# A two-layer mixture-of-experts image tower on one core: middle groups' rows given out two ahead, difference matrices one ahead, and a later wait on VectorE

## The chip, the cores and the metric

One NeuronCore of one Trainium2 chip runs the whole program. The metric is the device time of one execution in microseconds (us), taken as the median over runs of the same kernel on the same chip. The engines of the core each run their own instruction stream: TensorE (PE, with its weight loads PEld), VectorE (DVE), ScalarE (ACT), GpSimd (POOL) and SyncE (SP), which here only gives out transfers. ScalarE and GpSimd give out transfers too. The streams meet in semaphores: an instruction `wait_ge` stands in one engine's stream until another engine or a transfer has counted far enough, and everything behind it in that stream stands as well.

## The reference, cut to what matters

The input is 128 images of 3 x 224 x 224. Each image becomes 64 patches, each projected to 128 numbers, with a class token in front: 65 tokens an image, 8320 tokens in all. Two layers follow, each with a residual attention part and a residual mixture-of-experts part (all after a layer norm):

```
h = tokens(x) * pos_embed
h = h + attention0(norm(h))            # softmax attention within each image
h = h + experts0(norm(h))              # 32 experts, top 2, relu, hidden 128
h = h + attention1(norm(h))            # below
h = h + experts1(norm(h))              # 16 experts, top 2, gelu, hidden 512
```

The second attention is without softmax. For row t of an image it is

```
delta   = cumsum(h)[t] - h[t-1]                      # its norm is the magnitude
context = sum over s <= t of exp(-softplus(k) * (t - s)) * h[s]
result  = abs(norm2(delta) * context)
```

Both sums are matrix products along the token axis: `delta` with a matrix of zeros and ones ("difference"), `context` with a matrix `exp(rate * distance)`.

## The kernel before, in words

**Front stage.** The tokens are taken in 16 groups of 8 images (520 tokens). For each group the patch projection, the attention of layer 0, the router of layer 0 and the writing of every token's row, twice, into per-expert lists in DRAM run as a software pipeline over groups. The lists are written by GpSimd, ten indirect transfers a group (line 2061, "scatter"; semaphores `scattered`).

**Layer 0's experts.** 73 blocks of up to 256 list rows. SyncE and ScalarE each give out a part of each block's weights and rows (lines 597 and 599). The first 8 blocks are loaded before the lists are complete. From block 8 on the loads wait until everything is scattered and until padding rows have been written behind each list (`pads`, lines 566 to 574: SyncE writes 20 of them, ScalarE 8 and then 4; `dispatched`, line 577). PE transposes (line 910) and multiplies (926, 950), DVE applies relu (1813) and the gate (1861), GpSimd scatters the results back to DRAM (2089, semaphores `y_out`).

**Middle stage.** The tokens are taken again in 13 groups of 640, numbered 0 to 12. In this stage three transfers of 640 KB are given out by SyncE for each group g:

- its rows, two per token, as written by layer 0's experts (`rows_landed(g)`: waits until the results of all blocks that this group may need have landed, then for its buffer, `m_free`, counted by the sum of group g-2; line 627). There are two buffers, `yin` (in `x_hi` and `x_lo`). VectorE's `gather(g)` (line 1884) sums the two rows of a token and takes the norm's statistics.
- its difference matrix (`load_difference(g)`, line 658; waits for `delta_ps`, PE's delta product of group g-2; two buffers).
- its distance matrix (`load_distance(g)`, line 652; waits for `m_spread`, counted by ScalarE's `decays(g-1)`, line 1349; one buffer).

Groups' work overlaps. VectorE's `mid_step(g)` holds, in this order: the norm of group g's router input (`r1_apply`, 1462), `powers` (1901 to 1917), `gather(g+3)` (1884 to 1895), `mixed_in(g+1)` and its statistics (1923, 1452), the choice of experts of g (`r2`, 1570 to 1601), the gate of g (`r2_gate`, 1613 to 1617, which waits for ScalarE's exponentials), the ranks (`r3`, 1630, which waits for PE) and the slots (1645). ScalarE in the same step: `r1_x2T`, `absolute(g+1)` (1342), the copy of rows (1137), `normalized(g+2)` (1333), `guessB(g+1)`, `decays(g+2)` (1349, waits for the distance matrix), the exponentials for the router of g (1209, 1210), `squares(g+2)` (1312), `powers`. PE: `r1`, `r2`, `delta(g+2)` (1029, 1032), `r3` (829 to 835), `context(g+2)`. GpSimd then scatters group g's rows into layer 1's lists (2061, ten transfers).

The first middle groups are worked in among layer 0's last blocks: the table `EARLY` (line 412) gives the block at which step g (from -3 to 1) begins, and each engine's list `early` gives the offset of every piece. `LAST` is 1. Steps 2 to 12 follow as a plain loop once layer 0's blocks are done. On SyncE the early pieces are the rows up to group 4 and the matrices up to group 3; the rest is the loop that the diff touches.

**Layer 1's experts.** 81 blocks of up to 256 rows. The first four are loaded when ten groups' rows are in the lists; the rest wait, as in layer 0, for all scatters and for the pads. The last stage sums the two results of a token and stores the output.

Before layer 0's blocks VectorE waits (lines 1960 and 1961) until all scatters of layer 0 have landed, since the middle groups reuse the buffers these read. The first middle piece on VectorE is `gather(0)`, at block 47.

Of the kernel before, what the change touches and what calls it, by code (L numbers as in the profile page):

```python
# [31 lines left out]
GROUPS = 16  # L32
# [5 lines left out]
TILES = 5  # L38
ROWS = GT // TILES
HALF = GT // 2  # L40
TOP = 2
# [17 lines left out]
MG = TOKENS // (TILES * WIDE)  # L59
# [76 lines left out]
L0 = Layer(1, "L0", 32, 128, 256, 2, ROWS, GROUPS, [3, 7, 11, 15], 12, 8, 34)  # L136
# [124 lines left out]
def build(nc, a, out):  # L261
    ctx = ExitStack()
    with ctx:
# [149 lines left out]
        LAST = max(EARLY)  # L413
# [72 lines left out]
        S = {l.name: LayerSignals(sem, halves, l.name) for l in (L0, L1)}  # L486
# [119 lines left out]
        def sp_blocks(sp, l, behind=None):  # L606
            sp.wait_ge(T.tables_ready, 2 * l.turn - 1)
            for n, scattered in enumerate(S[l.name].scattered):
                sp.wait_ge(scattered, 16 * TILES * TOP * len(range(n, l.known, len(S[l.name].scattered))))
            for i in range(l.early):  # L610
                for part_ in range(l.parts):
                    load_part(sp, l, i, 0, part_)
            pads(sp, l, 0, PADS[l.name])
            dispatched(sp, l)

            def load(u, j):
                if l.unroll * j + u >= l.early:
                    load_part(sp, l, u, j, 0)
                    if l.mixed[l.unroll * j + u]:
                        load_part(sp, l, u, j, 2)  # L620
                if behind:
                    behind(l.unroll * j + u)

            rounds(sp, l, load)
# [7 lines left out]
        def _(sp):  # L632
# [10 lines left out]
            def load_rows(g):  # L643
                h, j = g % 2, g // 2
                if j > 0:
                    sp.wait_ge(m_free[h], j)
                sp_group_in(sp, "L0", g, h, yin, m_in[h])

            def load_distance(g):
                if g > 0:  # L650
                    sp.wait_ge(m_spread, g)
                sp.dma_start(m_dist[:, :, :].rearrange("p t c -> p (t c)"), a["distance"][g]).then_inc(dist_in, 16)

            def load_difference(g):
                h = g % 2
                if g > 1:
                    sp.wait_ge(delta_ps, g - 1)
                sp.dma_start(m_delta[h][:, :, :].rearrange("p t c -> p (t c)"), a["difference"][g])\
                    .then_inc(delta_in[h], 16)

            def mid_class(g):

                done = (g + 1) * TILES * WIDE - 1
                return L0.class_of(done // (TILES * ROWS))

            def landed(l, enough):

                for b in range(max(0, enough - NB), enough):
                    sp.wait_ge(K[l.name].y_out[b % NB], K[l.name].y0[b % NB] + 16 * (l.packets(b) + l.tiles_of(b)))

            def rows_landed(g):
                landed(L0, L0.enough(mid_class(g)))
                load_rows(g)
# [11 lines left out]
                    sp.wait_ge(chunk_used[h][c], GROUPS // 2)  # L685
            sp_blocks(sp, L0, among)
            among.left()
            for g in range(LAST + 3, MG):
                if g > LAST + 3:
                    rows_landed(g)  # L690
                load_distance(g)
                load_difference(g)

            def load_end(g, u, j):
                if j > 0:
# [721 lines left out]
        def _(dve):  # L1417
# [508 lines left out]
            def one_of(g):  # L1926

                return g if 0 <= g < MG else None
# [28 lines left out]
            dve.tensor_scalar(kcol[:, 1:2], kcol[:, 1:2], LEAST, -1.0, ALU.max, ALU.mult).then_inc(consts_dve, 1)  # L1957
            dve.memset(rows_mid[2][:, :, :, D:ROW], 0.0)

            for h in range(2):  # L1960
                dve.wait_ge(S["L0"].scattered[h], 16 * TILES * TOP * (GROUPS // 2))
            counts = {}

            def chosen_first(g):
                counts[g] = r2(L1, g, g % 2, g // 2)
# [8 lines left out]
            def early(g):  # L1974
                if g >= 0:
                    yield 0, r1_apply, L1, g, g % 2, g // 2
                if g + 2 >= 0:
                    yield 1, powers, g + 2, one_of(g + 1), g + 3
                yield 2, gather, g + 3
                if g + 1 >= 0:  # L1980
                    yield 3, mixed_in, g + 1
                    yield 3, r1, L1, g + 1, (g + 1) % 2, (g + 1) // 2
                if g >= 0:
                    yield 4, chosen_first, g
                    yield 6, slots_then, g

            among = Among(early)
            expert_blocks(L0, among)
            among.left()
# [186 lines left out]
```

## Time and profile before

| | |
|---|---|
| median of 3 runs | 1150.5 us (1148.85 to 1151.22) |
| profiled execution, first to last instruction (span) | 1146.4 us |
| profiled execution's own time | not given apart from its span; the span lies 4.1 us under the median |
| PE busy | 936.4 us, 82% |
| DVE busy | 876.0 us, 76% |
| POOL busy | 673.3 us, 59% |
| ACT busy | 511.0 us, 45% |
| moved by transfers | 246.60 MB, mean 215 GB/s |
| granted TensorE clock, mean | 0.889 |

The span runs through four stages: the front (0 to about 458 us), layer 0's experts (to about 692 us, with middle steps -3 to 1 in among them), the plain loop of middle steps (to about 848 us) and layer 1's experts (to the end). Shares of busy time are averages over these stages; each has another limit. All times in the rows are us from the span's start unless marked ns.

### The profile page before, as it was taken

Reading aid. Unit: us, or ns where it says so; the run is one execution under the profiler, and the core shown is the slowest. Engines: PE = TensorE matmul, PEld = TensorE weight load, DVE = VectorE, ACT = ScalarE, POOL = GpSimd, SP = SyncE. Lnnn points to the kernel's source line nnn. Section 1 sums busy time; section 2 is a strip of 40 time slices with the busy share of each in tenths; the row PEclk is TensorE's granted clock in tenths of the full one; section 3 lists DMA queues with packets and bytes.
Section 4 is the critical chain, followed back from the end, with each engine's and each line's share of the span. In section 5 each row is a group of like instructions: output and inputs, shape, how many; then the busy total and the mean of one; then the engine's idle time right before and its main releaser. Section 6 shows DMA issues by size and latency. Waiting matters only on the chain.

```text
span 1146.4 us, 21968 instructions
## 1 busy us (share of the span) xinstructions
PE 936.4 (82%) x6140; PEld 789.8 (69%) x6140; DVE 876.0 (76%) x3376; ACT 511.0 (45%) x1358; POOL 673.3 (59%) x622
## 2 busy tenths in 40 slices
PE   6999999999999973476667876566638999999992
PEld 2666676777667663466556765565638999999992
DVE  0588988988898966466678897677866888888883
ACT  1355555445555421111113545555524666656651
POOL 1036667666666633667777577766674545555552
PEclk9999999999999975678897887777759999999996
DMA  9856655666664032487789854455356888889886
GB/s 374 349 181 223 215 192 199 234 219 215 206 230 142 26 85 71 129 220 208 208 245 329 258 166 152 161 178 181 102 197 233 257 259 272 283 268 342 274 300 223
DMA packets 118667, 246.60 MB, mean 215 GB/s; under 512 B 20914, under 2 KB 85936, under 8 KB 112400
## 3 DMA queue, kind: packets, MB, share of 16 engines
q1 hardware_dynamic: 78016, 191.53, 50.6%
q0 software_dynamic: 18592, 34.68, 8.9%
q10 hardware_dynamic: 21936, 18.98, 5.5%
q8 instruction: 49, 0.80, 0.3%
q14 instruction: 74, 0.61, 0.2%
HBM read 201.68 MB, written 45.43 MB: 216 GB/s over the span
## 4 chain that ended last, share of the span: by engine, by line
PE 43%; DVE 22%; DMA 10%; issue 9%; SPq 7%; ACT 5%; POOL 3%; ACTq 1%; DVEq 0%; POOLq 0%
PE ps L950 11%; PE ps L931 9%; PE ps L734 4%; DMA x_hi<-results_L 3%; PE ps L801 3%; PE ps L785 3%; POOL lists_L L2061 2%; SPq L597 2%; SPq L599 2%; SPq L590 2%; DMA x_lo<-results_L 2%; PE ps L727 2%; PE ps L910 2%; PE ps L773 2%; PE ps L751 2%
## 5 line engine op out<-in xcount | busy, mean ns | idle before, releaser
L2061 POOL DMA_INDIRECT lists_L<-rows,slots x250 | 281.0, 1124 | 185.0 <-issue 173.1
L2089 POOL DMA_INDIRECT results_L<-xin x145 | 144.0, 993 | 122.7 <-DVE xin L1861 95.0
L2089 POOL DMA_INDIRECT results_L<-xin,place x146 | 143.8, 985 | 64.3 <-issue 39.5
L734 PE MATMUL ps<-xin,w_emb 128*128 128x512 f32 x292 | 138.2, 610 | 9.7 <-DMA w_emb<-in_w_main 8.6
L950 PE MATMUL ps<-xin,QK 128*128 128x128 f32 x838 | 115.3, 288 | 6.5 <-DVE QK L1813 4.4
L950 PEld LDWEIGHTS ps<-xin,QK 128*128 128x128 f32 x838 | 107.0, 203 | 8.0 <-DVE QK L1813 4.7
L931 PE MATMUL ps<-x_hi,x_lo 128*128 128x256 f32 (+1 forms) x324 | 98.5, 304 | 1.1 <-DVE x_lo L1829 1.1
L910 PE MATMUL ps<-ident,xin 128*128 128x128 f32 x291 | 65.9, 309 | 39.6 <-DMA xin<-lists_L 37.4
L2070 POOL TENSOR_TENSOR x_lo<-xin,x_hi 128x2048 fp32r<-128x2048 f32 x13 | 60.1, 4625 | 63.8 <-ACT x_hi L1118 63.5
L1271 ACT ACTIVATE QK<-ps,xin 128x256 f32<-128x256 f32 x164 | 64.4, 475 | 71.5 <-PE ps L931 71.5
L734 PEld LDWEIGHTS ps<-xin,w_emb 128*128 128x128 f32 x292 | 52.8, 194 | 59.2 <-issue 48.6
L931 PE MATMUL ps<-x_lo,x_hi 128*128 128x256 f32 (+1 forms) x324 | 92.5, 286 | 0.0
L931 PE MATMUL ps<-x_hi 128*128 128x256 f32 (+1 forms) x324 | 92.4, 285 | 0.0
L1835 DVE TENSOR_SCALAR xin<-xin 128x128 f32<-128x128 f32 x291 | 91.6, 361 | 0.6
L950 PE MATMUL ps<-xin,UH 128*128 128x128 f32 x648 | 89.8, 284 | 2.5 <-DVE xin L1861 2.1
L1137 ACT ACTIVATE h0T<-ps 128x256 f32<-128x256 f32 x73 | 27.9, 383 | 129.0 <-PE ps L910 108.3
L950 PEld LDWEIGHTS ps<-xin,UH 128*128 128x128 f32 x648 | 82.1, 198 | 4.0 <-issue 4.0
L1271 ACT ACTIVATE UH<-ps,xin 128x256 f32<-128x256 f32 (+1 forms) x160 | 55.5, 430 | 37.4 <-PE ps L931 37.4
L910 PEld LDWEIGHTS ps<-ident,xin 128*128 128x128 f32 x291 | 38.7, 157 | 47.8 <-DMA xin<-lists_L 44.8
L926 PE MATMUL ps<-h0T,xin 128*128 128x128 f32 (+1 forms) x326 | 59.2, 318 | 14.8 <-ACT h0T L1137 6.0
L926 PEld LDWEIGHTS ps<-h0T,xin 128*128 128x128 f32 x326 | 53.1, 235 | 17.5 <-issue 9.4
L931 PEld LDWEIGHTS ps<-x_hi,x_lo 128*128 128x128 f32 x324 | 63.3, 195 | 1.5 <-DVE x_lo L1829 1.5
(310 smaller groups left out, 2443.1 us busy)
## 6 DMA issues: line engine op xcount, KB each, us to landing
xin<-in_x_main SPq DMA_DIRECT2D x48, 1536.0 KB, 6.8
xin<-in_w_L SPq DMA_DIRECT2D x81, 578.0 KB
xin<-in_w_L SPq DMA_DIRECT2D x98, 128.0 KB
xin<-lists_L SPq DMA_DIRECT2D x64, 132.0 KB
xin<-in_w_L ACTq DMA_DIRECT2D x65, 128.0 KB
xin<-in_difference SPq DMA_DIRECT2D x13, 640.0 KB
xin<-in_distance SPq DMA_DIRECT2D x13, 640.0 KB
x_hi<-results_L SPq DMA_DIRECT2D x11, 640.0 KB, 5.9
```

The lines of the kernel that those rows point to most:

```text
L734: mm = pe.matmul(psE[h], w_emb[:, k, :], xin[h][c][:, n, :], start=(k == 0), stop=False, skip_group_check=True)
L785: mm = pe.matmul(pair[0][0:SEQ, i * D:(i + 1) * D], x1T[h][:, i * SEQ:(i + 1) * SEQ], wv[:, :], start=True, stop=True)
L801: mm = pe.matmul(pair[2][:, c:c + SEQ], V[h][:, i, :], Pr[h][:, i, :], start=True, stop=True)
L910: mm = pe.transpose(ps[:, banks(l, i)[0], q * 128:(q + 1) * 128], xblk[b][:, q, 0:D], ident[:, :])
L926: mm = pe.matmul(bank_h(i, f)[:, of_part], w1, xTb[p2][:, of_part], start=True, stop=True)
L931: mm = pe.matmul(bank_h(i, f)[:, 0:n_in], w[p2][:, cols_f], x[p2][:, 0:n_in], start=(n2 == 0), stop=(n2 == 2), skip_group_check=True)
L950: mm = pe.matmul(o, hTb[p2][:, f, rows_in], w2[:, f * D:(f + 1) * D], start=(f == 0), stop=(f == l.FC - 1))
L1271: ins = act.activation(hTb[p2][:, f, 0:n_in], ps[:, 2 + 2 * p2 + f // 2, f % 2 * l.block:f % 2 * l.block + n_in], ACT.Gelu, bias=b1)
L1835: ins = dve.tensor_scalar(xblk[u][:, q, 0:D], xblk[u][:, q, 0:D], xblk[u][:, q, SPREAD:SPREAD + 1], xblk[u][:, q, MEAN:MEAN + 1], ALU.mult ...
L2061: pool.indirect_dma_start(out=lists[l.name], out_offset=bass.IndirectOffsetOnAxis(ap=slots_of(l, g, h)[:, t, k:k + 1], axis=0), in_=buf[:, ...
L2070: pool.tensor_tensor(x_lo0[:, :, :].rearrange("p k n -> p (k n)"), xin[h][0][:, 0:KS, :].rearrange("p k n -> p (k n)"), x_hi0[:, :, :].rea ...
L2089: pool.indirect_dma_start(out=results[l.name], out_offset=bass.IndirectOffsetOnAxis(ap=where, axis=0), in_=yblk[u][:, q, :], in_offset=Non ...
```

## The change

SyncE's loop over the remaining middle groups gives out its transfers in another order, and each earlier. Before, for g from 4 to 12: rows of g (from 5 on), distance of g, difference of g. After: first rows of 5 and difference of 4; then for g from 4 to 12: rows of g+2, difference of g+1, distance of g. The waits inside each are the same. On VectorE the wait for layer 0's scatters moves from before layer 0's blocks to just before `gather(0)` at block 47.

```
             sp_blocks(sp, L0, among)
             among.left()
+            rows_landed(LAST + 4)
+            load_difference(LAST + 3)
             for g in range(LAST + 3, MG):
-                if g > LAST + 3:
-                    rows_landed(g)
+                if g + 2 < MG:
+                    rows_landed(g + 2)
+                if g + 1 < MG:
+                    load_difference(g + 1)
                 load_distance(g)
-                load_difference(g)
...
-            for h in range(2):
-                dve.wait_ge(S["L0"].scattered[h], 16 * TILES * TOP * (GROUPS // 2))
             counts = {}
+
+            def buffers_free():
+
+                for h in range(2):
+                    dve.wait_ge(S["L0"].scattered[h], 16 * TILES * TOP * (GROUPS // 2))
...
                     yield 1, powers, g + 2, one_of(g + 1), g + 3
+                if g == -3:
+                    yield 2, buffers_free,
                 yield 2, gather, g + 3
```

## Rows read from the trace of the kernel before

**Rows 1.** Line 1884, 700 to 812 us: what it waited for (us, times).
```profile
  DMA x_hi<-results_L: 11.3, 4
  DMA x_lo<-results_L: 9.5, 3
```

**Rows 2.** Chain that ended last, middle loop: start, us, what.
```profile
694.46 1.35 ACT xin L1349
...
696.94 7.92 DMA x_hi<-results_L
...
704.88 0.83 DVE atok L1884
```

**Rows 3.** Timeline of SP: start, us, engine, line, transfer.
```profile
657.31 20.51 SPq L652 DMA_DIRECT2D xin<-in_distance  x2
...
695.83 0.33 SPq L652 DMA_DIRECT2D xin<-in_distance  x1
```

**Rows 4.** Page, transfers by line: count, size, median us to landing.
```profile
x_hi<-results_L SPq DMA_DIRECT2D x11, 640.0 KB, 5.9
```

**Rows 5.** Busy time by stretch: length, PE, PEld, DVE, ACT, POOL, clock, DMA share, GB/s.
```profile
704.88:717.58 12.70, 8.06 (x51) 7.34 (x51) 11.57 (x70) 5.39 (x22) 9.65 (x11) 0.76 0.47 151
688.50:701.94 13.44, 9.15 (x61) 8.57 (x61) 11.72 (x72) 8.43 (x30) 10.32 (x11) 0.75 0.46 146
```

**Rows 6.** Timeline of DVE: gate, ranks and slots of step 2; slots of 9, 10, 12.
```profile
696.63 0.23 DVE L1613 TENSOR_REDUCE gsum<-lgs 128x5 f32<-128x80 f32 x1
...
697.74 0.39 DVE L1630 TENSOR_TENSOR pick<-ps,oh 128x80 f32<-128x80 f32 x2 [0.25 <-PE ps L835]
...
698.72 0.17 DVE L1645 SCALAR_TENSOR_TENSOR slots<-chosen,rank 128x10 uint32<-128x10 f32 x1
...
809.23 0.17 DVE L1645 SCALAR_TENSOR_TENSOR slots<-chosen,rank 128x10 uint32<-128x10 f32 x1
...
824.27 0.17 DVE L1645 SCALAR_TENSOR_TENSOR slots<-chosen,rank 128x10 uint32<-128x10 f32 x1
...
847.63 0.17 DVE L1645 SCALAR_TENSOR_TENSOR slots<-chosen,rank 128x10 uint32<-128x10 f32 x1
```

**Rows 7.** Timeline of PE, step 2: delta, ranks, context.
```profile
692.90 0.80 PE L1029 MATMUL ps<-xin 128*128 128x128 f32 x2 [2.52 <-ACT xin L1333]
...
697.33 0.23 PE L829 MATMUL ps<-ohs,before 128*128 128x80 bf16 x1
...
698.05 0.39 PE L1029 MATMUL ps<-xin,xin 128*128 128x128 f32 x2
```

**Rows 8.** Timeline of POOL: last result of layer 0; scatters of groups 2 and 5.
```profile
691.98 0.98 POOL L2089 DMA_INDIRECT results_L<-xin,place  x1 [0.30 <-issue]
...
705.99 0.97 POOL L2061 DMA_INDIRECT lists_L<-w_emb,slots  x1 [0.30 <-issue]
...
748.00 0.97 POOL L2061 DMA_INDIRECT lists_L<-w_emb,slots  x1 [3.85 <-DVE slots L1645]
```

**Rows 9.** Line 2061, 705 to 865 us: landing of its scatters.
```profile
DMA to landing us min/median/max: 2.3/2.8/8.2
```

**Rows 10.** Chain that ended last, at the start of layer 1's experts.
```profile
862.80 3.49 DMA lists_L<-rows,slots
```

**Rows 11.** Timeline of SP at that start: the pads.
```profile
850.08 13.10 SPq L574 DMA_DIRECT2D lists_L<-padrows  x16
```

**Rows 12.** Timeline of PE at the start of layer 1's experts.
```profile
871.58 0.69 PE L910 MATMUL ps<-ident,xin 128*128 128x128 f32 x2 [4.88 <-DMA xin<-lists_L]
```

**Rows 13.** Timelines of DVE, ACT and SP at the start of layer 0's experts.
```profile
474.25 0.42 DVE L1813 TENSOR_SCALAR QK<-ps 128x256 f32<-128x256 f32 x1 [8.12 <-DMA lists_L<-rows,slots]
...
471.49 5.39 ACTq L574 DMA_DIRECT2D lists_L<-padrows  x8
...
460.42 16.18 SPq L574 DMA_DIRECT2D lists_L<-padrows  x20
```

**Rows 14.** Chain that ended last, at the start of layer 0's experts.
```profile
479.95 2.08 DMA lists_L<-padrows
```

## The prediction

> **What bounds the kernel now.** I read the waits of the middle loop first, then the chain of waits there, then the timelines of SP, DVE, ACT, PE and POOL side by side for one step, and last the two places where an expert stage starts.
>
> In the middle loop VectorE stops once in each of steps 3 to 9, always before line 1884, the sum of the rows of groups 6 to 12. The reader is to see seven waits, 11.3 + 9.5 = 20.8 us together, all for a rows transfer [rows 1]. The chain shows why: `decays` of one step ends (694.46 + 1.35 = 695.81), SyncE then passes its wait, gives out distance, difference and rows within 1.1 us, and the rows, third in line, land at 704.86; the sum starts at 704.88 [rows 2]. So every step holds a loop: sum, statistics, `decays`, three transfers, sum. Nothing but program order on SyncE ties the rows to `decays`. Their buffer has been free since the sum two groups back.
>
> Between slots of group 2 (698.72) and of group 9 (809.23) lie 110.5 us, seven steps of 15.8 us [rows 6]. Without its wait, step 3 holds 12.70 us of VectorE work from one sum to the end of the next `powers` [rows 5]; over the seven steps it is (110.5 - 20.8) / 7 = 12.8 us.
>
> GpSimd follows. It needs 10 sends a group; in the stretch of 12.70 us it makes 11 with 9.65 us busy and 0.3 us between them [rows 5, 8], so some 12.7 us a group. Late in the loop it waits for VectorE's slots, 3.85 us at 748.00 [rows 8]. Behind the loop the whole delay reaches the end: the last scatter is sent at 862.80 and lands 3.49 us later, SyncE's next loads go out, and PE, which had stood 4.88 us, starts again at 871.58 [rows 10, 12]. From there on PE is the bound to the end, so a time saved at this restart is saved at the end.
>
> **The change part by part.**
>
> (a) *Rows two ahead.* After the change the rows of g+2 are given out once the sum of g is done, more than a step before they are needed, where a 640 KB transfer takes 5.9 us to land [rows 4]. All seven waits go: -20.8 us. Bounds: 0 (if something holds SyncE longer than a step) and 20.8; I take 20.8, as the slack is a full step. No instruction is added on SyncE: the same transfers, in another order.
>
> (b) *What is late next.* PE's order in a step is delta, then ranks, then context. In step 2, which had no wait for rows, delta started at 692.90, ran 4.4 us, the ranks followed at 697.33 with nothing between, and VectorE stood before 1630 [rows 6, 7]. So step 2 is the pattern of a step without the row wait, and it lasted 13.44 us, from 688.50 to 701.94 [rows 5], 0.6 more than 12.8. Seven steps of 13.44 are 94.1 us: together (a) and (b) give 110.5 - 94.1 = 16.4. Bounds of (b): 0 and 0.74 a step (against step 3's own 12.70), so (a) and (b) are worth 15.6 to 20.8.
>
> GpSimd at 12.7 us a group stays just under 13.44 and is no bound.
>
> In those steps the clock granted to PE matters: a pair of delta's matmuls took 0.80 us, of the context products behind it 0.39 [rows 7], the two levels of 1.2 and 2.4 GHz. The Trainium skill (TensorE: Matmul & The Clock Gate, "Part 1: The HAM clock gate") says that the slow clock is the default and that sustained activity releases it; by this a loop without the row wait might keep the fast clock. The trace speaks against it: step 2 had no row wait and its delta still ran slow. It stands below as a rival.
>
> (c) *The first distance matrix.* This goes the other way. Before, the distance of group 4 was given out as soon as `decays(3)` was done, as the second of the two transfers of [rows 3] that end at 677.8, and `decays(4)` could run at 694.46 [rows 2]. After the change SyncE must first give out the rows of group 6. Group 6 lies in the third class of layer 0's tokens, which needs all 73 blocks' results in DRAM. The last of these is sent by GpSimd at 691.98 [rows 8]; a scatter lands 2.8 us after its send at the median, 2.3 at least [rows 9]: about 694.8. So SyncE stands from about 659 (657.31 and two more transfers given out) to 694.8, and the distance of 4 is queued behind it. Before, this wait cost nothing, as the rows of 6 were asked for at 696.94 [rows 2].
>
> Then rows 6, difference 5 and distance 4 go out together. Three such transfers took from 695.83 [rows 3] to 704.86 [rows 2], 9.0 us. Distance 4 lands at about 703.8, and `decays(4)` starts 9.3 us later than before. Behind it on ScalarE stand the exponentials for the router, which VectorE's gate at 696.63 awaits. Between the end of `decays` (695.81) and that gate there were 0.8 us [rows 2, 6], with the exponentials in them, so the slack is between 0 and 0.8; I take 0.5. VectorE, GpSimd and all behind come 8.8 us later. Bounds: if the transfer needed only the 5.9 us of [rows 4] after 694.3, `decays` would start 5.7 later, 5.2 on the path; if the five transfers that can then be in flight (rows 7 and difference 6 follow at once) share the rate evenly, 9.0 x 5/3 = 15 us, so 14.8 on the path. I take 8.8, since the three in front are exactly the pattern measured.
>
> The Trainium skill (DMA: Bandwidth & Descriptors, "Queues, rings and completion order") says that each DMA engine consumes the descriptors of a ring in order, so distance 4 would wait for the two in front and not for the two behind. The same page's fit, 2.0 us plus bytes over 436 GB/s ("Anatomy of one DMA"), would be an estimate of 6.5 us for the three instead of the 9.0 measured, and the forecast would be 2.5 us lower; the measured number is used.
>
> (d) *Difference one ahead.* Difference g+1 stands before distance g and waits for delta of g-1. Counted from the start of the sum, step 2's delta ended at 697.33 - 688.50 = 8.8 us and its `decays` at 7.3 [rows 2, 5, 7], so distance g goes out some 2 us later than it could, at about 9.3. It is wanted at the next `decays`, at 13.4 + 6.0 = 19.4, so it has 10.1 us to land. Two transfers in line take between 5.9 (one) and 9.0 (three) [rows 2 to 4]. Cost 0, cover 1 us at least; if it is gone, every step pays (rival 3).
>
> (e) *End of the loop.* Steps 10 to 12 have no sum; from slots 9 to slots 12 they take 38.4 us [rows 6] as before. The last send came 15.2 us after slots 12 [rows 6, 10], GpSimd being behind. After the change it has run dry before slots 10 and starts level: two groups of 12.7 and nine sends of 1.27 put the last send 36.8 us after slots 10 (824.27), which is 13.4 us after slots 12 [rows 6], 1.8 closer. The pads, 850.08 + 13.10 = 863.2 plus 2.1 of landing, then are last, at 865.3 against the old 866.3 [rows 10, 11, 14]. Gain 1.0, bounds 0 and 1.8.
>
> (f) *VectorE's wait.* It was 8.12 us before the first relu [rows 13]. Taking it away lets blocks 0 to 2 run some 5 us earlier. Block 8's loads don't follow: they went out when ScalarE's second set of pads had landed, 479.95 + 2.08 = 482.0 [rows 14], and these stood behind its own first eight, 471.49 to 476.9 [rows 13], not behind VectorE. From there SyncE's issue of loads is the chain. Value 0. Bounds: a gain of 3.4 if the loads could start when SyncE's pads (460.42 + 16.18, plus 2.1) have landed; nothing below 0, since at block 47 the scatters have been in for 100 us.
>
> Sum: -16.4 + 8.8 - 1.0 = -8.6 us. The profiled span of 1146.4 becomes 1137.8; what lies around it is 4.1 us against the median, so the time is 1150.5 - 8.6 = 1141.9.
>
> **The rivals.**
>
> 1. *Distance 4 is not on the path* (it lands soon, or the wait for the exponentials is absorbed by the backlog of GpSimd). GpSimd came to group 2's rows at 705.99 [rows 8] though its slots were ready at 698.9 [rows 6], so 7 us of a delay would not reach it if VectorE could catch up. Against: without row waits VectorE has no slack of its own. Time 1150.5 - 16.4 - 1.0 = 1133.1. Chance 0.10.
>
> 2. *PE's clock stays up through delta.* Delta's 4.4 us would be 2.2, so the stop in (b) vanishes: 7 x 0.63 = 4.4 us more. Against it stands step 2. Time 1137.5. The section on the clock gate of the Trainium skill (TensorE: Matmul & The Clock Gate), named above, is the case for it. Chance 0.10.
>
> 3. *Distance becomes the bound in every step: slower.* It now goes out behind difference, after delta. If it landed later than the next `decays` wants it, each of eight steps would stand. By (d) the point is a landing time of 10.1 us. Before, three transfers took 9.0. With scatters and the next rows in between, 12 us would cost 1.9 x 8 = 15 us: 1150.5 - 8.6 + 15 = 1157. It is slower by over 0.2% when it costs 11 us, from a landing of 11.5 on. Against: only two transfers are in line. Chance 0.08.
>
> 4. *The row wait goes but another stands in its place at the same time* (SyncE reaches the rows late, the loop keeps 15.8 us): -1 to +2 from the order alone, about 1150.5. For it speaks that program order still ties rows of g+3 behind distance g; against it that distance g goes out before the next sum is even done. Chance 0.07.
>
> My forecast, 1138.5 to 1145.5, has 0.60; the remaining 0.05 is a gain from (f) on top, to 1138.4 at best, or a delay between the cases.
>
> **How the numbers follow.** The time is that of the forecast, 1141.9. What a measurement of this kernel can tell from no change is about 0.2%, 2.3 us. Faster holds forecast, rivals 1 and 2 and the rest: 0.85. Same is rival 4: 0.07. Slower is rival 3: 0.08. The range reaches from rival 1 (1133) to where the bound of (c) ends, 6.0 us above the forecast: 1133 to 1148.
>
> **What the profile of the changed kernel would show.** No wait before line 1884 in groups 7 to 12. Slots 2 to slots 9 in about 94 us. SyncE standing from about 659 to 695 before line 627, then five transfers in 3 us. `decays(4)` at about 703.8, not 694.5, and VectorE standing some 9 us before line 1613 once. Layer 0's experts unchanged to 1 us, with the first relu near 468. PE's restart near 863 instead of 871.6. Wrong: a wait for the distance transfer in later steps, a step longer than 14 us, or `decays(4)` near its old place.

## The result, and the profile after

The changed kernel took 1142.74 us at the median (1138.16 to 1144.18, 7 runs), the kernel before 1148.86 us beside it on the same chip (1145.53 to 1151.73, 7 runs). The ratio is 0.9946, 95% interval 0.9927 to 0.9964: 6.2 us faster, between 4.1 and 8.4. The forecast was 1141.9 us, a ratio of 0.9925 to its own baseline of 1150.5. So the sign, the time and the range came out; the gain was forecast 2.4 us too large. The profiled execution took 1138.16 us (span 1136.4), the shortest of the seven. Its span is 10.0 us under the span before, and part of that difference is not the change's: layer 0's last result is sent at 689.17 there and at 691.98 before [rows 8]. No run below shows a cause for that (see the section on SyncE's and VectorE's parts). Times in the middle stage are therefore best counted from that send.

Lines have moved by the edit: 1884 is now 1887, 1349 is 1352, 1613 is 1616, 1630 is 1633, 1645 is 1648, 1029 is 1032, 829 is 832, 2061 is 2069, 2089 is 2097, 910 is 913. Lines 574 to 658 are where they were.

**The row wait is gone.** The sums of line 1887 from 690 to 840 us (against [rows 1]); under "sat idle" the view would list what they waited for:

```profile
L1887 DVE TENSOR_TENSOR atok<-x_hi x2: 818/818/818, 706.6 to 788.3; 128x640 f32<-128x640 f32 x2
...
its engine sat idle before it (us, times) until:
who waited for it (us, times):
```

**What VectorE waits for now.** The waits of DVE from 690 to 840 us: for what, us in total, times, longest.

```profile
DVE gsum L1616 <- ACT eg L1213: 9.0, 1, 9.0
DVE pick L1633 <- PE ps L838: 5.8, 7, 1.1
```

The seven stops of 3.0 us for rows have become seven of 0.8 us for the ranks, and one of 9.0 us for ScalarE's exponentials. The timeline of DVE shows that one, and the slots of groups 2, 9, 10 and 12 (against [rows 6]):

```profile
701.77 0.24 DVE L1616 TENSOR_REDUCE gsum<-lgs 128x5 f32<-128x80 f32 x1 [8.98 <-ACT eg L1213]
...
703.53 0.17 DVE L1648 SCALAR_TENSOR_TENSOR slots<-chosen,rank 128x10 uint32<-128x10 f32 x1
...
798.88 0.17 DVE L1648 SCALAR_TENSOR_TENSOR slots<-chosen,rank 128x10 uint32<-128x10 f32 x1
...
813.90 0.17 DVE L1648 SCALAR_TENSOR_TENSOR slots<-chosen,rank 128x10 uint32<-128x10 f32 x1
...
837.28 0.17 DVE L1648 SCALAR_TENSOR_TENSOR slots<-chosen,rank 128x10 uint32<-128x10 f32 x1
```

Slots 2 to slots 9 took 95.35 us where they took 110.5. The step ahead of them, from the sum of group 5 (684.57) to the sum of group 6 (706.64), took 22.07 us where it took 13.44 [rows 5].

**Where the 9 us come from.** The timeline of SP (against [rows 3]) and the line of `decays` in that of ACT:

```profile
656.56 0.52 SPq L658 DMA_DIRECT2D xin<-in_difference  x1
691.90 0.38 SPq L627 DMA_DIRECT2D x_hi<-results_L  x1
692.34 0.51 SPq L658 DMA_DIRECT2D xin<-in_difference  x1
692.90 0.42 SPq L652 DMA_DIRECT2D xin<-in_distance  x1
693.63 0.53 SPq L627 DMA_DIRECT2D x_lo<-results_L  x1
```

```profile
700.11 1.36 ACT L1352 ACTIVATE xin<-xin,kcol 128x1280 f32<-128x1280 f32 x1 [9.48 <-DMA xin<-in_distance]
```

SyncE gives out nothing from 657 to 691.90. What ends that is GpSimd's last result of layer 0, sent at 689.17. The chain that ended last passes through it:

```profile
689.17 2.58 DMA results_L<-xin,place
...
692.90 7.19 DMA xin<-in_distance
700.11 1.37 ACT xin L1352
```

The distance matrix of group 4 is the third transfer given out from 691.90 on, and lands 8.2 us after the first of the three was given out.

**GpSimd.** Its timeline: the last result, the first scatters of groups 2, 3 and 10, and the last scatter of all (against [rows 8]).

```profile
689.17 0.98 POOL L2097 DMA_INDIRECT results_L<-xin,place  x1 [0.30 <-issue]
...
704.68 0.97 POOL L2069 DMA_INDIRECT lists_L<-w_emb,slots  x1 [1.80 <-DVE slots L1648]
...
718.48 0.97 POOL L2069 DMA_INDIRECT lists_L<-rows,slots  x1 [1.19 <-DVE slots L1648]
...
815.07 0.97 POOL L2069 DMA_INDIRECT lists_L<-rows,slots  x1 [2.56 <-DVE slots L1648]
...
852.48 0.97 POOL L2069 DMA_INDIRECT lists_L<-rows,slots  x1 [0.30 <-issue]
```

Before, it came to group 2's rows 7 us after their slots were ready. Now it has run dry by then, and it stands before nearly every group. PE starts layer 1's experts at 860.75 (against [rows 12]):

```profile
860.75 0.69 PE L913 MATMUL ps<-ident,xin 128*128 128x128 f32 x2 [4.98 <-DMA xin<-lists_L]
```

From there to the end of the span it is 275.6 us, and before it was 274.8; no run explains the 0.8 between them.

### The profile page after: what moved, and what is told of

Same layout as the page of the kernel before. It is cut to its first block, busy times and chain, and to the rows that moved or that the text cites. A ratio compares the mean times of both kernels' runs of the same rounds, so it can differ in the third digit from the quotient of the medians.

```text
span 1136.4 us, 21968 instructions
## 1 busy us (share of the span) xinstructions
PE 931.7 (82%) x6140; PEld 788.5 (69%) x6140; DVE 877.4 (77%) x3376; ACT 511.2 (45%) x1358; POOL 675.7 (59%) x622
## 4 chain that ended last, share of the span: by engine, by line
PE 47%; DVE 20%; issue 10%; ACT 6%; SPq 6%; DMA 6%; POOL 4%; ACTq 1%; DVEq 0%; POOLq 0%
PE ps L953 12%; PE ps L934 10%; PE ps L737 4%; PE ps L804 3%; POOL lists_L L2069 3%; PE ps L788 2%; PE ps L1032 2%; SPq L599 2%; PE ps L761 2%; SPq L590 2%; SPq L597 2%; PE ps L1035 2%; PE ps L913 2%; PE ps L730 2%; PE ps L776 2%
## 5 line engine op out<-in xcount | busy, mean ns | idle before, releaser
L953 PE MATMUL ps<-xin,QK 128*128 128x128 f32 x838 | 118.2, 293 | 2.4 <-DVE xin L1864 2.3
L953 PEld LDWEIGHTS ps<-xin,QK 128*128 128x128 f32 x838 | 109.8, 207 | 4.3 <-issue 4.2
```

Of the source, the lines that this page charges most:

```text
L953: mm = pe.matmul(o, hTb[p2][:, f, rows_in], w2[:, f * D:(f + 1) * D], start=(f == 0), stop=(f == l.FC - 1))
```

## The experiments

All ratios are against the kernel before on the same chip. The kernels ran on several chips, so two of them are better compared by their ratios than by their medians. The table holds what each profile (one execution) shows of the middle stage: T is GpSimd's last result of layer 0, "last scatter" its last send into layer 1's lists, "stood" the idle time from 684 us on that the view of GpSimd's waits puts down to slots (a plain gap of 0.3 us between sends counts where the slots came last, and a longer one that the view calls "issue" does not).

| kernel | ratio (95%) | T | T to last scatter | stood |
|---|---|---|---|---|
| before | 1 | 691.98 | 170.8 | 19.4 in 8 |
| VectorE's part alone | 1.0003 (0.9983 to 1.0023) | 692.71 | 170.3 | 17.6 in 6 |
| before, ranks split | 1.0027 (1.0007 to 1.0047) | 691.13 | 171.3 | 19.0 in 6 |
| changed | 0.9946 (0.9927 to 0.9964) | 689.17 | 163.3 | 10.5 in 8 |
| SyncE's part alone | 0.9939 (0.9923 to 0.9954) | 690.99 | 164.4 | 11.8 in 8 |
| changed, GpSimd more | 0.9945 (0.9927 to 0.9964) | 688.80 | 163.0 | 5.0 in 3 |
| changed, ranks split | 0.9925 (0.9900 to 0.9951) | 689.90 | 162.4 | 8.1 in 5 |
| distance second | 0.9926 (0.9900 to 0.9952) | 688.46 | 160.8 | 6.9 in 6 |
| results first | 0.9914 (0.9896 to 0.9931) | 682.82 | 167.4 | 1.2 in 4 |
| distance first, GpSimd more | 0.9902 (0.9883 to 0.9920) | 691.51 | 157.5 | 0.9 in 3 |
| rows alone | 0.9892 (0.9875 to 0.9910) | 690.69 | 155.3 | 0.9 in 3 |
| distance first, ranks split | 0.9872 (0.9841 to 0.9903) | 695.37 | 155.1 | 0.9 in 3 |
| distance first | 0.9866 (0.9850 to 0.9883) | 691.83 | 155.0 | 0.9 in 3 |

### SyncE's part alone, VectorE's part alone

The first leaves the wait of line 1960 before layer 0's blocks, where it was, and takes only SyncE's new loop. The second takes only this:

```
-            for h in range(2):
-                dve.wait_ge(S["L0"].scattered[h], 16 * TILES * TOP * (GROUPS // 2))
             counts = {}
+            def buffers_free():
+                ... (the same two waits)
 ...
+                if g == -3:
+                    yield 2, buffers_free,
                 yield 2, gather, g + 3
```

> SyncE's new order alone, VectorE's wait at the head of layer 1 left where it was before. My theory (the prediction's steps (a) to (e)): all of the gain is SyncE's, so the ratio to the kernel before is that of the whole change, 0.994 to 0.996 (about 1143 us), the gather starts of the middle groups are 13.6 us apart and the first distance matrix still lands late (gate of group 4's decays some 8 to 9 us behind). Rival: VectorE's moved wait is worth the 2 to 3 us by which layer 0's last stage ended earlier in the profile of the changed kernel; then this kernel is 2 to 3 us slower than the changed one, about 1145 to 1146, and GpSimd's first result of the first layer-1 pass comes at about 477 us and not at 472.

> VectorE's moved wait alone, SyncE's order as before. My theory (step (f) at zero): ratio 0.999 to 1.001, seven waits of the gather for the row transfers, 21 us together, as before. Rival: the wait is worth 2 to 3 us, because VectorE's first products of layer 1 no longer stand behind the last scatter of layer 0's lists: ratio 0.9975 to 0.998, about 1146 us, with the slots of group 0 near 659 us where the kernel before had them at 662.5.

SyncE's part alone took 1140.77 us, ratio 0.9939, with the stop of 8.6 us before the gate and seven of 0.9 us for the ranks. VectorE's part alone took 1148.74, ratio 1.0003, with the seven row waits back (21 us). The whole gain is SyncE's, within what these intervals tell. VectorE's move does reach something. These are GpSimd's first results of layer 0's experts (the expectations above call them layer 1's), first with VectorE's part alone, then with SyncE's part alone:

```profile
472.19 1.00 POOL L2094 DMA_INDIRECT results_L<-xin,place  x1 [0.96 <-DVE xin L1861]
```

```profile
476.53 1.00 POOL L2092 DMA_INDIRECT results_L<-xin,place  x1 [6.02 <-DVE xin L1864]
```

The first blocks finish 4.3 us sooner, and nothing comes of it: the rows of block 8 (line 599) were asked for at 482.44 and at 481.95 us, that is, no sooner in the kernel with the move. The slots of group 0, at 659.2 in the changed kernel's profile and 662.5 before, stand at 662.8 with the move alone and at 661.6 without it. So VectorE's move alone doesn't bring the earlier end of layer 0 that the changed kernel's profile has. Nor is it shown to be chance. The five profiles that have VectorE's move and let the distance matrix of group 4 wait for the rows of group 6 have group 0's slots at 658.6 to 660.5, the eight others at 661.2 to 665.9. Yet "distance first", which is among the eight, gives out the same transfers in the same order up to the difference matrix of group 4, at the head of SyncE's long stand. In those five the profiled execution was also a quick one, 1.7 to 4.6 us under its kernel's median; in the others with such a time on record it lies between 1.6 under and 0.8 over. What makes the middle stage start early in them stays open. In the changed kernel's profile it is 3.9 of the 10.0 us between the spans.

### Distance first

```
             load_difference(LAST + 3)
+            load_distance(LAST + 3)
             for g in range(LAST + 3, MG):
                 if g + 2 < MG:
                     rows_landed(g + 2)
                 if g + 1 < MG:
                     load_difference(g + 1)
-                load_distance(g)
+                    load_distance(g + 1)
```

> The changed kernel with one thing moved: each distance matrix is given out with its group's difference matrix, one group ahead, so that the first one (group 4) stands ahead of the rows of group 6 on SyncE. My theory (step (c)): the one wait of 9 us ahead of ScalarE's decays of group 4 goes, the second step of the gather is 13 to 14 us and not 22, and the time falls by 8 to 9 us to 1133 to 1135, ratio 0.986 to 0.988 to the kernel before. Rival A: another wait stands just behind the removed one (the rows of group 6 themselves, or the scatter of group 1's lists): the second step becomes 16 to 20 us and the time 1136 to 1141. Rival B: the distance, now a whole group earlier on the same queue, delays the rows that the gather needs: waits of the gather on its rows come back, 1 to 3 us a step, and the time is that of the kernel before or more.

It took 1132.82 us (1131.94 to 1133.12, 4 runs), ratio 0.9866: 9.9 us less than the changed kernel by the medians, 9.2 by the ratios. The timeline of SP shows the distance of 4 leaving at 677.39, in the middle of the long stand:

```profile
658.37 0.58 SPq L658 DMA_DIRECT2D xin<-in_difference  x1
677.39 0.33 SPq L652 DMA_DIRECT2D xin<-in_distance  x1
694.16 0.38 SPq L627 DMA_DIRECT2D x_hi<-results_L  x1
```

The gate's stop is gone, and the second step took 13.17 us (688.56 to 701.73). The stops for the ranks are still there, as the waits of DVE from 690 to 860 show:

```profile
DVE pick L1634 <- PE ps L839: 5.2, 7, 0.8
```

But they no longer decide. The waits of POOL from 692 to 848 us:

```profile
POOL lists_L L2070 <- issue: 35.7, 117, 0.3
POOL lists_L L2070 <- DVE slots L1649: 0.9, 3, 0.3
```

No gap before the last scatter is longer than 0.3 us. GpSimd sends without a pause from layer 0's last result to its last scatter, 155.0 us. The chain of the page, by line, says it too: the scatters hold 10% of the span here and 3% in the changed kernel.

```profile
PE ps L954 11%; POOL lists_L L2070 10%; PE ps L935 9%; PE ps L738 4%; PE ps L805 3%; PE ps L789 3%; SPq L599 2%; SPq L597 2%; SPq L590 2%; PE ps L914 2%; PE ps L731 2%; PE ps L777 2%; DMA xin<-lists_L 2%; PE ps L755 2%; DVE bnB L1456 2%
```

### Rows alone

```
             rows_landed(LAST + 4)
-            load_difference(LAST + 3)
             for g in range(LAST + 3, MG):
+                load_distance(g)
+                load_difference(g)
                 if g + 2 < MG:
                     rows_landed(g + 2)
-                if g + 1 < MG:
-                    load_difference(g + 1)
-                load_distance(g)
```

> Rows two groups ahead, but distance and difference of a group given out together and ahead of the rows, as one loop: no matrix is one group ahead of the kernel before. My theory (steps (a), (c) and (d)): the matrices' being ahead is worth nothing, only that the rows are ahead and that the first distance matrix does not stand behind rows that wait: 1133 to 1135, the same as with the distance given out first. Rival: the difference matrix one group ahead is needed, because TensorE's delta of the group waits for it once the rows go first: then this kernel is 1 to 3 us a step (5 to 20 us in all) slower than the one with the distance given out first, with waits of TensorE's delta on that transfer.

It took 1135.23 us (1133.70 to 1136.05, 4 runs), ratio 0.9892, 2.4 us more than distance first on the same chip. The intervals of the two ratios overlap, but each of its four runs is above each of the four of distance first, so the 2.4 us may be real. The middle stage doesn't show them: T to last scatter is 155.3 us against 155.0, and PE has no wait for a difference matrix. The difference matrices' being one ahead is worth nothing there; where the 2.4 us would come from is open.

### The distance second in line

```
                 if g + 2 < MG:
                     rows_landed(g + 2)
+                load_distance(g)
                 if g + 1 < MG:
                     load_difference(g + 1)
-                load_distance(g)
```

> The changed kernel with the order in each step of rows(g+2), distance(g), difference(g+1) in place of rows, difference, distance: of the transfers that SyncE gives out at once when the last results of layer 0 are in, the first distance matrix is second and not third. If the transfers of one queue are served in order (my step (c) took the third to land 9 us after the first was given out), it lands 2 to 3 us earlier and the time falls by 2 to 3 us to 1140, the wait of VectorE before the gate of group 4 being 6 to 7 us and not 9.0. If they share the rate evenly, it lands where it did: 9 us, 1142 to 1144.

1138.93 us, ratio 0.9926, under the changed kernel by 3.8 us of the medians and 2.3 of the ratios; the intervals overlap, and the traces have to settle it. The timelines of SP and ACT:

```profile
691.07 0.38 SPq L627 DMA_DIRECT2D x_hi<-results_L  x1
691.50 0.51 SPq L652 DMA_DIRECT2D xin<-in_distance  x1
692.06 0.43 SPq L658 DMA_DIRECT2D xin<-in_difference  x1
```

```profile
697.56 1.36 ACT L1352 ACTIVATE xin<-xin,kcol 128x1280 f32<-128x1280 f32 x1 [7.64 <-DMA xin<-in_distance]
```

Second in line it lands 6.5 us after the first was given out, third in line 8.2, and the gate stood 7.1 us, not 9.0. T to last scatter fell by 2.5 us. The 8.2 us are the shortest of five profiles in which it was third: the others have 9.1 (changed, GpSimd more), 9.4 (changed, ranks split), 9.5 (SyncE's part alone) and 9.2 (results first). So place in the queue counts, by 1.7 to 3.0 us here, with one profile of the second place; even sharing would not show it. The Trainium skill (DMA: Bandwidth & Descriptors, "Queues, rings and completion order") has it that each DMA engine takes the descriptors of one ring in order; these traces agree.

### The layer's results first

```
-                        yield 6 + n // TOP, send, L1, g, g % 2, n, n + TOP
+                        yield 90 + n // TOP, send, L1, g, g % 2, n, n + TOP
```

> The changed kernel, SyncE's order untouched, but GpSimd sends the lists of groups 0 and 1 (twenty scatters) behind all of layer 0's results and not among the last of them. My theory for step (c): SyncE stands at the rows of group 6 until layer 0's last result is in DRAM, so the late first distance matrix moves with the time T of GpSimd's last result send: some 8 to 12 us earlier than 689, which makes VectorE's 9 us before the gate of group 4 shrink by as much, to 0 to 1 us. Then GpSimd holds the end, 130 scatters of 1.28 us from T on: last send at T + 167, which is 846 to 852, and the time is 1132 to 1138. Rival: SyncE waits there for a buffer or for VectorE's sum, not for the results; then the gate still stands 8 to 9 us and the time is 1142 or more.

With this edit GpSimd's pieces for groups 0 and 1 move behind all of layer 0's results. It took 1137.14 us, ratio 0.9914. T moved from 689.17 to 682.82, less than the 8 to 12 us that I expected. SyncE's stand ended with it, 2.4 us behind (2.7 in the changed kernel), and the gate's stop shrank from 9.0 to 3.3 us, by 5.7 us for the 6.4 us of T, and so not to the 0 to 1 us expected. The timeline of SP, and the waits of DVE from 660 to 860 us:

```profile
656.36 0.52 SPq L658 DMA_DIRECT2D xin<-in_difference  x1
685.22 0.38 SPq L627 DMA_DIRECT2D x_hi<-results_L  x1
```

```profile
DVE gsum L1616 <- ACT eg L1213: 3.3, 1, 3.3
DVE rows L1465 <- DMA lists_L<-rows,slots: 2.7, 1, 2.7
```

So SyncE waits for the results, not for a buffer. The last scatter comes at T + 167.4, as expected for 130 scatters and no pause. The second line is a price that I had not put down: `rows` buffers are reused after three groups, and with group 0's scatters held back VectorE waits for them once.

### The ranks split from delta

The same edit on three kernels (the kernel before, the changed one, distance first), here as it stands in the middle loop:

```
                 if g + 2 < MG:
-                    delta(g + 2)
+                    delta(g + 2, 0, 3)
                 r3(L1, g, g % 2, g // 2)
                 if g + 2 < MG:
+                    delta(g + 2, 3, TILES)
```

> The changed kernel with the same move of the ranks in TensorE's order. Here GpSimd has run dry after the late first distance matrix and stands 0.7 us a step before VectorE's slots, so my theory (step (b) is on the path in this kernel and the stop is the ranks behind a slow delta): the stop of 5.8 us in all goes, steps become 12.7 to 12.8 us until GpSimd's own 12.7 holds, and the time falls by 4 to 5 us to 1138 to 1139, ratio to the kernel before 0.990 to 0.991. Rival: the stop moves to delta's second part and the context products, ScalarE's squares come late, and nothing is gained: 1142 to 1144.

> The kernel with the distance given out first (1132.8 us, middle steps of 13.55 us), and in TensorE's order of a middle step the ranks moved between tiles 0 to 2 and tiles 3 and 4 of delta, so that they no longer stand behind all of it. My theory now: in that kernel GpSimd is the bound from before the middle loop to the last scatter (no gap over 0.3 us between its sends from 681 to 847 us), VectorE's stop of 0.8 us a step for the ranks lies beside it, so taking the stop away is worth nothing: 1131.5 to 1134, with VectorE's steps near 12.7 us and the last send of GpSimd where it was (within 1 us of 847), only further behind the last slots (20 us and not 15). Rival: VectorE with TensorE is the bound there, as the prediction had it for the changed kernel: 5 to 6 us faster, 1127 to 1128.

> The kernel before with the same move of the ranks alone. My theory: there the ranks waited behind delta in the group 2 step only, and the wait for the rows (3 us a step) hides everything else, so ratio 0.999 to 1.001. Rival: earlier ranks bring the decays, the three transfers and thus the next sum forward, since they are one loop: up to 0.5 us a step, 3 to 4 us, ratio 0.997.

On the kernel before nothing is gained: ratio 1.0027 (1.0007 to 1.0047), outside the 0.999 to 1.001 that I expected and on the slow side, with the row waits in place; where the loss comes from is not shown. On distance first, 1135.05 us against 1132.82 (ratios 0.9872 and 0.9866, overlapping). Two of its six runs took 1129.3 and 1129.4 and four 1134.8 to 1135.9; the profile is of one of the four. The stops for the ranks are gone from its waits, but slots 2 to slots 9 took 93.8 us and not 94.8, so its steps are 13.4 us and not the 12.7 expected. T to last scatter is 155.1 against 155.0: GpSimd bounds that kernel, as expected. (Its last scatter is at 850.4, outside the "within 1 us of 847" that I expected; its T is later by the same 3.5 us.)

On the changed kernel the median is the one expected, 1138.79 us, but the ratio of 0.9925 is not (0.990 to 0.991), and T to last scatter fell by 1.0 us only, where the removed stops were 5.8 us. The steps from slots 2 to slots 9 are the seven windows of this table (length; busy us of PE, PEld, DVE, ACT, POOL with counts; granted clock; DMA share; GB/s):

```profile
705.11:717.70 12.59, 8.82 (x53) 8.20 (x52) 11.48 (x70) 6.66 (x18) 8.85 (x9) 0.64 0.43 142
717.70:730.44 12.74, 8.95 (x63) 8.32 (x62) 11.62 (x71) 8.45 (x29) 9.69 (x10) 0.76 0.62 209
730.44:743.66 13.22, 9.37 (x63) 8.75 (x62) 11.78 (x71) 8.45 (x29) 10.07 (x10) 0.76 0.60 202
743.66:758.02 14.36, 11.04 (x63) 10.58 (x62) 11.87 (x71) 8.45 (x29) 11.09 (x11) 0.62 0.56 189
758.02:771.33 13.31, 9.23 (x63) 8.61 (x62) 11.72 (x70) 8.45 (x29) 9.56 (x9) 0.76 0.59 195
771.33:785.57 14.24, 10.92 (x63) 10.41 (x62) 11.94 (x71) 8.45 (x29) 10.93 (x11) 0.62 0.42 145
785.57:798.59 13.02, 9.22 (x64) 8.60 (x63) 11.69 (x71) 8.45 (x29) 9.15 (x9) 0.76 0.52 160
```

Without its stop a step can take 12.6 to 12.7 us. In two steps the granted clock was 0.62 and not 0.76, PE was busy at least 1.5 us longer with as many matmuls, and the step took 14.3 us. (The first window, at 0.64, holds 53 matmuls and not 63, as much of its work lay ahead of it.) In these two steps context ran at the slow level too, with pairs of 0.64 us as in the line below, where in the four steps at 0.76 they mostly take 0.39:

```profile
746.28 0.64 PE L1035 MATMUL ps<-xin,xin 128*128 128x128 f32 x2
```

From slots 2 to slots 9 VectorE stood 1.7 us in these two steps for ScalarE's `xin`, and 1.6 us in five steps for its `guessC`, which comes behind context; neither stop is there between these slots in the changed kernel. The mean step is 13.35 us against 13.62, 1.9 us in seven. So part of the rival held: new stops of 3.3 us, behind delta's second part and context, stand where the old ones of 5.8 us were, and VectorE was busy 0.6 us longer. The medians' 4 us (2.4 by the ratios) and the trace's 1.0 us can't all be the effect, and the intervals don't decide; what the split is worth here is open between 1 and 4 us.

### GpSimd given more to do

```
             for g in range(LAST + 1, MG):
                 send(L1, g, g % 2)
+                if g < MG - 1:
+                    for n in range(3 * g, 3 * g + 3):
+                        pool.memset(... 50 columns of x_lo0 each ...)
```

> The kernel with the distance given out first, and three small memsets on GpSimd behind the scatters of each of groups 2 to 11 (some 0.2 us each with the gap, 0.6 a group, 6 us in all), which nothing waits for. My theory that GpSimd never stands idle in this kernel between the end of layer 0 and its last scatter: nearly all of it reaches the end, 5 to 6.5 us slower than that kernel, 1138 to 1139. Rival, VectorE's steps of 13.55 us are the bound (GpSimd has 0.8 us a group over): 1133 to 1134.

> The changed kernel with the same memsets. GpSimd there stands some 0.7 us before the slots of each group 3 to 9, so my theory is that they lie in that idle time and only those behind the last two or three groups cost anything: 1 to 2 us slower than the changed kernel, 1143.5 to 1145. Rival, GpSimd bounds this kernel as well: 6 us slower, 1148 to 1149.

The dose was smaller than planned, as the timeline of POOL shows on distance first:

```profile
717.74 0.97 POOL L2070 DMA_INDIRECT lists_L<-w_emb,slots  x1 [0.30 <-issue]
718.71 0.31 POOL L2120 MEMSET x_lo<- 128x50 f32 x3
719.19 0.97 POOL L2070 DMA_INDIRECT lists_L<-rows,slots  x1 [0.17 <-issue]
```

Three memsets put the next send 1.45 us behind the last and not 1.27: 0.18 us a group, 1.8 us in ten groups. On distance first T to last scatter rose by 2.5 us (155.0 to 157.5) and the ratio from 0.9866 to 0.9902, touching intervals. The time of 1136.23 us lies between the two expectations, for the dose was a third of the planned one.

On the changed kernel the time stayed (ratio 0.9945 against 0.9946, where 1 to 2 us more were expected), and T to last scatter was 163.0 us against 163.3. Where the memsets went shows in GpSimd's timeline. Behind them the view calls the rest of a wait for slots "issue":

```profile
731.62 0.31 POOL L2119 MEMSET x_lo<- 128x50 f32 x3
732.61 0.97 POOL L2069 DMA_INDIRECT lists_L<-rows,slots  x1 [0.69 <-issue]
```

So the 5.0 us in the table leave out five such stops of 3.2 us in all. In the changed kernel GpSimd stood 11.2 us before its groups, 0.7 of them called "issue"; with the memsets it stood 8.2 us and spent 3.1 in memsets, 11.3 together. The memsets lie in its idle time, as far as the profile can tell. With a dose of 1.8 us the times alone would not carry the verdict; the counted stops do.

## Why the prediction was right, point by point

(a) *Rows two ahead*: right in full. All seven waits are gone, as in the kernel with SyncE's part alone.

(b) *What is late next*: the mechanism was right, the size a little low. The ranks stood behind a slow delta, 0.83 us a step and not 0.63; steps took 13.62 us and not 13.44. Together (a) and (b) gave 110.5 - 95.35 = 15.2 us where 16.4 were forecast. PE's clock in the changed kernel falls as it did in [rows 7]: in the step shown the granted clock was 0.50 over delta (711.40 to 715.80) and 1.00 over context (716.60 to 718.50). Delta's pairs took 0.63 to 0.79 us, context's behind them 0.39 (timeline of PE):

```profile
711.39 0.79 PE L1032 MATMUL ps<-xin 128*128 128x128 f32 x2 [2.52 <-ACT xin L1336]
711.97 0.63 PE L1035 MATMUL ps<-xin 128*128 128x128 f32 x2
...
715.81 0.27 PE L832 MATMUL ps<-ohs,before 128*128 128x80 bf16 x1
...
717.22 0.39 PE L1032 MATMUL ps<-xin,xin 128*128 128x128 f32 x2
```

So rival 2 is wrong, and with it the case for a fast clock that the prediction took from the Trainium skill (TensorE: Matmul & The Clock Gate, "Part 1: The HAM clock gate"). What that section of the Trainium skill states, that activity releases the slow clock, is not contradicted: PE had stood 2.52 us before this delta, and the clock was up again behind it.

(c) *The first distance matrix*: right in mechanism and size. The step took 8.6 us longer where 8.8 were forecast. SyncE went on 2.7 us after the last result's send, where 2.8 were taken; third in line took 8.2 us in this profile and 9.1 to 9.5 in four others, where 9.0 were taken. (The prediction quotes a fit beside it, of 2.0 us plus bytes over 436 GB/s. The Trainium skill, in DMA: Bandwidth & Descriptors, "Anatomy of one DMA", states it for transfers given out by GpSimd, and these are SyncE's; none of the five profiles shows its 6.5 us for three.) Three runs show the cause from three sides: the distance given out ahead of those rows (stop gone), second and not third (stop 7.1), results sent earlier (stop 3.3). Rival 1 is wrong for this kernel.

What I missed is beside the sum. "GpSimd ... is no bound" is true of the changed kernel only because of (c). It enters the loop with a backlog of 7 us [rows 6, 8]. At 12.7 us a group it works that off by 0.9 us a step against VectorE's 13.6, so without the late distance it never runs dry, and VectorE's stops for the ranks lie beside its work. The 9 us stop let it run dry at 704, and from then on it waited for VectorE before every group up to 10. So (b) and (c) are no independent terms. With (c) out of the way the kernel costs 1132.8 us, where rival 1's sum gave 1133.1. That agreement is in part luck: what bounds this kernel is another engine than that sum assumed, and against the kernel before beside it the gain was 15.4 us and not 17.4.

(d) *Difference one ahead*: right, 0, as far as the middle stage shows it in rows alone; the 2.4 us between that kernel's median and that of distance first have no place in the trace. No distance matrix is waited for in a later step: rival 3 is wrong, and no other wait took the rows' place at the same time, which is rival 4.

(e) *End of the loop*: half of it came. I had the last scatter 36.8 us after slots 10; it came 38.6 us after (813.90 to 852.48) and 15.2 us after slots 12, exactly as before [rows 6, 10]. The step that failed is "it has run dry before slots 10 and starts level": it had run dry before as well, standing 2.61 us there and 2.56 now. And a start needs 1.2 us from the slots to the first send (813.90 to 815.07), which the sum left out; the remaining 0.6 us are single sends longer than 0.97 (one of 1.43 at 844.37). So the scatters, and not the pads, were last: the last one landed 3.06 us after its send, at 855.54, where it took 3.49 before, and that, not the loop, is nearly all of why PE's restart came 61.87 us after slots 9 and not 62.35. The gain was 0.5 us where 1.0 was forecast.

(f) *VectorE's wait*: right, 0. The first relu came at 468.07, as forecast, the block 8 loads where they were, and the part alone measured 1.0003.

Summed as measured: -15.2 + 8.6 - 0.5 = -7.1 us up to PE's restart, where -8.6 were forecast: 1.2 too much in (a) and (b), the 0.2 us a step; 0.5 too much in (e); and 0.2 too little in (c). Layer 1's experts then took 0.8 us longer, which no term foresaw and one profile can't tell from variation: -6.3 us, beside the measured -6.2 (4.1 to 8.4). The remaining 3.9 us of the 10.0 us between the two spans lie ahead of the sum of group 5 (684.57 against 688.50).

## What to carry to other kernels

Giving a transfer out earlier moves everything behind it on that queue: ask of each one what the new first in line waits for, and who waits for the next one behind it. Here a wait on layer 0's last result took 8.6 of 15.2 us, and putting one small line ahead of it gave them back (1132.8 us). And before a stop on one engine is priced at its length, look at the engine that it feeds: as long as that one has a backlog, the stop costs nothing, and once it has run dry, it can cost up to its length. How much it does cost is then still to be measured: of 5.8 us of stops, the split gave back between 1 and 4.

## What the runs showed of the hardware

- GpSimd's scatters left 1.27 us apart (0.97 busy and 0.30 between) for 155 us on end in distance first, with single sends of up to 1.6 us. Ten a group make 12.7 us.
- Of 640 KB transfers given out on SyncE within 1.1 us, the second landed 6.5 us (one profile) and the third 8.2 to 9.5 us (five) after the first was given out.
- Shorter steps did not bring PE's fast clock in delta: its granted clock was 0.50 without the row wait (711.40 to 715.80, changed kernel). With the ranks split, two of seven steps were granted 0.62 and not 0.76, and took some 1.3 us longer.
- Executions of one kernel differ by up to 9 us (before, 1142.29 to 1151.62 in 17 runs). Part of the difference between profiles lies ahead of the middle loop: T lay between 688.5 and 695.4 us in the twelve kernels that send layer 0's results in the same order. The three without VectorE's moved wait (690.99, 691.13, 691.98) lie in the midst of them, but the four that have it and the changed kernel's wait on SyncE are the four earliest (688.46 to 689.90), for a reason that no run shows.
